# Cross-attention of a decoder layer: both batches of a tile taken together, in halves of the TensorE array

## The chip, the cores and the metric

The kernel runs on one core of a Trainium2 chip. The metric is device time in microseconds (us) of one execution. The engines are named as the profile names them: PE (TensorE, its weight loads as PEld), DVE (VectorE), ACT (ScalarE), POOL (GpSimd), SP (the queue that issues DMAs).

## The reference, cut to what matters

`x` and `ctx` are (32, 64, 512): 32 batches of 64 channels and 512 positions. Three sublayers follow each other, each `x = layernorm(x + f(x))` over the last axis: an attention over batches (called "messages" below), a cross-attention, and a feed-forward network (FFN) with fake-quantised weights and activations. The change is in the second:

```
qh = einsum('bcn,oc->bon', x1, Wq)   # (b, 8 heads, 64, 512)
kh = einsum('bcn,oc->bon', ctx, Wk)
vh = einsum('bcn,oc->bon', ctx, Wv)
qh = softmax(qh, axis=-2) * SCALE    # over the 64 entries of a head
kh = softmax(kh, axis=-1)            # over the 512 positions
context = einsum('bhdn,bhen->bhde', kh, vh)
out = einsum('bhde,bhdn->bhen', context, qh)      # -> (b, 512, 512)
out = einsum('bcn,oc->bon', out, Wo) + bo         # -> (b, 64, 512)
y = out / max(sqrt(sum(out*out, axis=1)), 1e-12) * g * sqrt(64)
x2 = layernorm(x1 + y)
```

## The kernel before

Everything is kept in SBUF. `xt` holds x as 16 tiles (T = 16) of 128 partitions, which are the 64 channels of two batches, by 512 positions. The kernel is written as one instruction list for each engine, in an order set by hand; semaphores (`then_inc`, `wait_ge`) tie the lists. An engine takes its list strictly in order, so what stands behind a waiting instruction waits too.

The stages are: loads and quantisation of the FFN's weights; messages, into which the rest of the weight work is woven; cross-attention; FFN.

Cross-attention goes batch by batch: `slot(b, par, t)` handles batch b (half `par` of tile t) in a loop over t of two slots. While batch b is finished, the logits of batch b+1 are made. The steps of one batch:

- `logits` makes, for each of four 128-row pieces i, key logits into bank i % 2 (L1204) and query logits into bank 4 + i % 2 (L1211). The weights of the keys are padded with zeros, so that all 128 partitions of `ctxs` go through the array although only one batch counts. The query side is fp16 in two parts: `x1p` holds a high and a low half of x1 on the two partition halves, `Wq2` the same of Wq. To get x1 there, `keep_x1` copies it, four DMAs (L388) spread it over the partitions (`x1d`), `high_x1` and `split_x1` (L465) make the parts.
- `maxima` on DVE: negated key maximum (L705), query maximum for each head (L709), subtraction into `EQ` (L712). `exps` on ACT: key exponential with its sum (L960), query exponential (L963). `q_sum` (L718) and one reciprocal (L722) on DVE, `norm_p` on POOL (L475).
- `transpose_k` (L1223) and `transpose_p` (L1234) turn EK and EQ in 128x128 blocks through banks 2 and 3; `copy_k` and `copy_p` on ACT bring them to `ET` and `PTs`.
- `a_product` (L1240) = ctx times ET, over 4 pieces; ACT copies one half of the rows to `ATs`. G = ATs times `Bs` (Wo and Wv multiplied ahead) in L1301; `scale_g` (L742) divides by the key sums.
- `y_product` (L1247) makes y with the positions on the partitions, 64 columns at a time; `bias_y`, `norm_y` (POOL), `sum_y`; `transpose_y` (L1255, L1270) turns y of both batches back and `add_y` (L749) adds it to the tile.
- Layer norms: `ln_stats` (L688, L689) and `ln_apply` (L695) on DVE, the power on POOL. x2's quantisation for the FFN (`scale_x`, `quantize_x`) is woven in; `keep_xq` copies its result.

Of the kernel before, what the change touches and what calls it, by code (L numbers as in the profile page):

```python
# [8 lines left out]
ALU = mybir.AluOpType  # L9
# [42 lines left out]
def decoder_kernel(nc, x, ctx_in, Wq, Wk, Wv, Wo, bo, g, w_gate, w_up, w_down, out):  # L52
# [21 lines left out]
    with ExitStack() as stack:  # L74
# [33 lines left out]
        AREA = 29264  # L108
# [67 lines left out]
        xqn = cut(L // 2).bitcast(BF16)  # L176
# [15 lines left out]
        shift = cut(1)  # L192
        neg_mean = cut(1)
        zero = cut(1)
# [5 lines left out]
        s.q_max_ready = sem("q_max_ready")  # L200
        s.q_max_transposed = sem("q_max_transposed")
        s.q_scales_ready = sem("q_scales_ready")
        s.q_scales_spread = sem("q_scales_spread")
        s.q_scales_copied = sem("q_scales_copied")
        s.q_scaled = sem("q_scaled")
        s.q_high_ready = sem("q_high_ready")
        s.q_low_ready = sem("q_low_ready")
# [31 lines left out]
        s.ln_rstd = sem("ln_rstd")  # L239

        s.x1_ready = sem("x1_ready")
        s.x1n_ready = sem("x1n_ready")
        s.x1d_loaded = sem("x1d_loaded")
        s.x1_high_ready = sem("x1_high_ready")
        s.x1_split = sem("x1_split")
        s.ctx_loaded = sem("ctx_loaded")
# [10 lines left out]
        s.kT_ready = sem("kT_ready")  # L257
        s.kT_copied = sem("kT_copied")
# [4 lines left out]
        s.pqT_ready = sem("pqT_ready")  # L263
        s.pqT_copied = sem("pqT_copied")
        s.y_ready = sem("y_ready")
        s.y_biased = sem("y_biased")
        s.y_squared = sem("y_squared")
        s.y_ss = sem("y_ss")
        s.y_normed = sem("y_normed")
        s.yT_ready = sem("yT_ready")  # L270
        s.x2_added = sem("x2_added")
        s.x2_ready = sem("x2_ready")

        s.x_scaled = sem("x_scaled")
        s.x_shifted = sem("x_shifted")
        s.xqn_ready = sem("xqn_ready")
# [42 lines left out]
        def x1_index(t):  # L319

            return 1 if isinstance(t, int) and t == 0 else 2 * t

        def x2_index(t):

            return 2 * T - 2 if isinstance(t, int) and t == T - 1 else 2 * t + 1

# [9 lines left out]
        def _(sp):  # L336
# [3 lines left out]
            sp.dma_start(wkn[:, :, C:2 * C], Wk.rearrange("(t p) c -> p t c", p=P)).then_inc(s.small_loaded, 16)  # L340
            sp.dma_start(wvn, Wv.rearrange("(t p) c -> p t c", p=P)).then_inc(s.small_loaded, 16)
            sp.dma_start(won, Wo).then_inc(s.small_loaded, 16)
            sp.dma_start(bo_all[:], bo.rearrange("(a c) -> a c", a=1).to_broadcast([P, C])).then_inc(s.small_loaded, 16)
            for h in range(2):
                sp.dma_start(g8[C * h:C * h + C, :], g.rearrange("a c b -> (a c) b")).then_inc(s.small_loaded, 16)
# [38 lines left out]
            def load_x1d(t):  # L384
                sp.wait_ge(s.x1n_ready, t + 1)
                for b in range(2):
                    for h in range(2):
                        sp.dma_start(x1d[C * h:C * h + C, b], x1n[C * b:C * b + C]).then_inc(s.x1d_loaded, 16)  # L388
            sp.dma_start(ctxs, ctx_tok[0]).then_inc(s.ctx_loaded, 16)
            load_x1d(0)  # L390
            with sp.Fori(1, T) as t:
                load_x1d(t)
                sp.wait_ge(s.klog_ready, 8 * t)
                sp.wait_ge(s.ctxT_ready, t)
                sp.dma_start(ctxs, ctx_tok[t]).then_inc(s.ctx_loaded, 16)
# [6 lines left out]
        def _(pool):  # L402
# [9 lines left out]
            pool.memset(wkn[:, :, 0:C], 0.0).then_inc(s.consts, 1)  # L412
            pool.memset(wkn[:, :, 2 * C:3 * C], 0.0).then_inc(s.consts, 1)
            pool.memset(ones[:], 1.0).then_inc(s.consts, 1)
            pool.wait_ge(s.small_loaded, 16 * 8)
# [24 lines left out]
            pool.wait_ge(s.q_high_ready, 1)  # L440
            pool.tensor_tensor(Wq2[:, 1], Wqs[:], Wq2[:, 0], ALU.subtract).then_inc(s.q_low_ready, 1)
# [14 lines left out]
            def ln_rsqrt(n):  # L456

                pool.wait_ge(s.ln_var, n + 1)
                ch.link(pool.tensor_tensor(vare[:], mv[:, 1:2], eps_tile[:], ALU.add))
                pool.tensor_tensor(rstd[:], vare[:], minus_half[:, 0:1], ALU.pow).then_inc(s.ln_rstd, 1)  # L460

            def split_x1(b, par):

                pool.wait_ge(s.x1_high_ready, b + 1)
                pool.tensor_tensor(x1p[C:P, par], x1d[C:P, par], x1p[C:P, par], ALU.subtract).then_inc(s.x1_split, 1)  # L465

                pool.wait_ge(s.x1_split, b + 1)

            def norm_p(b, par):

                pool.wait_ge(s.q_rec_ready, b + 1)
                for i in range(NT):
                    e = EQ[:, par, i].rearrange("p (h d) -> p h d", d=DH)
                    r = qsum[:, par, HEADS * i:HEADS * (i + 1)].unsqueeze(2).to_broadcast([P, HEADS, DH])
                    pool.tensor_tensor(e, e, r, ALU.mult).then_inc(s.p_ready, 1)  # L475
# [7 lines left out]
            def norm_y(b, par):  # L483

                y = Ysb[:, :, C * par:C * par + C]
                pool.wait_ge(s.y_biased, b + 1)
                pool.tensor_tensor(Ysq, y, y, ALU.mult).then_inc(s.y_squared, 1)
                pool.wait_ge(s.y_ss, b + 1)
                ch.link(pool.tensor_tensor(yrn, yss, minus_half[:], ALU.pow))
                pool.tensor_tensor(y, y, yrn.unsqueeze(2).to_broadcast([P, NT, C]), ALU.mult).then_inc(s.y_normed, 1)  # L490

            def slot(b, par, t, front=True, y=True):
                ahead = par == 0 and not (isinstance(t, int) and t == T - 1)
                if ahead:
                    ln_rsqrt(x1_index(t))
                if y:
                    norm_y(b - 1, 1 - par)
                if par == 1 and not (isinstance(t, int) and t == 0):  # L500
                    shift_x(t - 1)

                if not y:
                    pool.wait_ge(s.ln_rstd, x1_index(t) + 1)
                elif par == 0 or (isinstance(t, int) and t == 0):
                    pool.wait_ge(s.y_normed, b)
                else:
                    pool.wait_ge(s.x_shifted, t)
                if not (isinstance(t, int) and t == T - 1):
                    split_x1(b + 2, par)  # L510
                if par == 0 and y:
                    ln_rsqrt(x2_index(t))
                if front:
                    norm_p(b + 1, 1 - par)
            ln_rsqrt(0)
            pool.wait_ge(s.ln_rstd, 1)
            for b in range(2):
                split_x1(b, b)
            norm_p(0, 0)
            slot(0, 0, 0, y=False)  # L520
            slot(1, 1, 0)
            with pool.Fori(1, T - 1) as t:
                ch.enter(t - 1, 4)
                slot(2 * t, 0, t)
                slot(2 * t + 1, 1, t)
            ch.leave(T - 2)
            slot(2 * T - 2, 0, T - 1)
            slot(2 * T - 1, 1, T - 1, front=False)
            norm_y(2 * T - 1, 1)


            def ln_shift(t):
# [27 lines left out]
        def _(dve):  # L560
# [126 lines left out]
            def ln_stats(src):  # L687
                ch.link(dve.bn_stats(st6[:], src), alone=True)  # L688
                dve.bn_aggr(mv[:], st6[:]).then_inc(s.ln_var, 1)  # L689
# [716 lines left out]
```

## Time and profile before

| | |
|---|---|
| median of 3 runs | 1008.78 us (1008.75 to 1013.59) |
| span of the profiled execution, first to last instruction | 1010.8 us |
| busy over the span | PE 80%, DVE 75%, ACT 56%, POOL 43% |
| mean granted clock of TensorE | 0.894 of full |
| messages' and weights' stages end, cross-attention starts | 213.6 us |
| first matmul of the FFN | 801.67 us |
| longest pause of PE after that | 815.2 to 822.6 us, until the first hidden tile is quantised |

The profiled execution's span is 2.0 us above the median of the timed runs and inside their range. In the rows below times are in us from the span's start, "x4" counts instructions that a row merges, and the bracket at a row's end is idle time of the engine just before it, with what ended it. "128*32" of a matmul is rows by columns of the array in use.

### The profile page before, as it was taken

To read this page: it belongs to the slowest core of one execution; us is meant where nothing else is said; L and a number is where in the kernel's file an instruction comes from. 1 tells how busy PE (TensorE), PEld (TensorE's weight loads), DVE (VectorE), ACT (ScalarE), POOL (GpSimd) and SP (SyncE) were. 2 spreads that over 40 slices of the span, in tenths; PEclk is the share of its full clock that TensorE was granted. 3 is DMA by queue.
4 is the path that set the end of the run, shared out by engine and by line. 5 is a ranking of instruction groups with operands and counts; after the bars stand their busy time and mean duration, and the time that the engine had idled before them with its cause. 6 is when DMAs were issued, how large, how long until landed. Compare 5 with 4: busy or idle time off the path is not lost.

```text
span 1010.8 us, 17612 instructions
## 1 busy us (share of the span) xinstructions
PE 809.3 (80%) x5463; PEld 545.3 (54%) x5463; DVE 759.0 (75%) x1660; ACT 568.5 (56%) x1051; POOL 437.1 (43%) x491
## 2 busy tenths in 40 slices
PE   2115555548999999999999999999999867778873
PEld 2104555524767676676766667676667633333331
DVE  3766777748788888888888888888888266666663
ACT  1119777636666666766666676666667223333332
POOL 4423333313445455454545545454553334444443
PEclk7557676659999999999999999999999789999997
DMA  8993111101001101101100110110010000000000
GB/s 201 204 200 137 32 31 31 37 21 32 14 19 31 22 9 31 31 1 30 31 21 10 31 31 0 31 31 21 10 31 1 1 1 30 23 21 21 21 21 31
DMA packets 30372, 38.77 MB, mean 38 GB/s; under 512 B 4496, under 2 KB 16784, under 8 KB 30352
## 3 DMA queue, kind: packets, MB, share of 16 engines
q1 hardware_dynamic: 30352, 38.51, 15.9%
q8 instruction: 12, 0.20, 0.1%
q14 instruction: 8, 0.07, 0.0%
HBM read 25.92 MB, written 4.19 MB: 30 GB/s over the span
## 4 chain that ended last, share of the span: by engine, by line
PE 58%; issue 14%; POOL 8%; DMA 8%; DVE 6%; ACT 5%; SPq 1%; POOLq 0%; ACTq 0%; DVEq 0%
PE bank L1247 11%; PE bank L1204 11%; PE bank L1240 11%; PE bank L1223 5%; PE bank L1170 5%; PE bank L1211 5%; ACT big L873 4%; PE bank L1234 4%; DMA big<-in_ctx_dram 4%; POOL big L545 3%; POOL rstd L540 3%; DMA big<-in_L_ffn_w_down_dram 2%; PE bank L1301 2%; DMA big<-in_L_ffn_w_up_dram 2%; DVE big L565 1%
## 5 line engine op out<-in xcount | busy, mean ns | idle before, releaser
L873 ACT ACTIVATE big<-bank 128x512 f32<-128x512 f32 (+4 forms) x368 | 195.3, 588 | 53.1 <-PE bank L1223 31.5
L475 POOL TENSOR_TENSOR big<-big 128x512 f32<-128x512 f32 x128 | 131.5, 1057 | 81.1 <-DVE big L722 81.1
L1204 PE MATMUL bank<-big,WkT 128*128 128x512 f32 x256 | 136.2, 614 | 13.0 <-DMA big<-in_ctx_dram 8.8
L873 ACT ACTIVATE big<-big 32x256 f32<-32x256 f32 (+6 forms) x160 | 120.3, 772 | 15.6 <-DVE big L766 9.9
L963 ACT ACTIVATE big<-big,q_scales 128x512 f32<-128x512 f32 x128 | 92.4, 722 | 64.3 <-DVE big L712 64.3
L960 ACT ACTIVATE big<-bank,big 128x512 f32<-128x512 f32 x128 | 87.7, 685 | 68.6 <-DVE big L705 67.5
L1247 PEld LDWEIGHTS bank<-big 128*128 128x128 f32 x1024 | 120.6, 194 | 5.6 <-DVE big L742 1.2
L1247 PE MATMUL bank<-big 128*128 128x64 f32 x1024 | 119.4, 275 | 1.0 <-DVE big L742 1.0
L1240 PE MATMUL bank<-big 128*128 128x512 f32 x256 | 116.7, 598 | 0.5 <-ACT big L873 0.5
L718 DVE TENSOR_REDUCE big<-big 128x8 f32<-128x512 f32 x128 | 87.1, 680 | 25.7 <-ACT big L963 24.7
L705 DVE TENSOR_REDUCE big<-bank 128x1 f32<-128x512 f32 x128 | 88.2, 689 | 17.5 <-PE bank L1204 14.4
L1170 PE MATMUL bank<-big 128*128 128x128 f32 x256 | 55.9, 407 | 54.5 <-ACT big L873 54.5
L712 DVE TENSOR_TENSOR big<-bank,big 128x512 f32<-128x512 f32 x128 | 88.5, 691 | 6.9
L709 DVE TENSOR_REDUCE big<-bank 128x8 f32<-128x512 f32 x128 | 87.0, 680 | 7.4 <-PE bank L1211 7.4
L465 POOL TENSOR_TENSOR big<-big 64x512 f16<-64x512 f32 x32 | 37.0, 1157 | 116.1 <-ACT big L873 116.0
L1073 ACT ACTIVATE big<-big,rstd 128x512 f32<-128x512 f32 x16 | 13.0, 812 | 125.1 <-POOL big L541 125.1
L1211 PE MATMUL bank<-Wq,big 128*128 128x512 f16 x256 | 76.7, 381 | 7.2 <-POOL big L465 7.2
L1170 PEld LDWEIGHTS bank<-big 128*128 128x128 f32 x256 | 51.6, 308 | 56.6 <-issue 32.9
L545 POOL TENSOR_TENSOR big<-big 128x1376 f32<-128x1376 f32 x16 | 40.1, 2508 | 93.5 <-DVE big L569 93.5
L1240 PEld LDWEIGHTS bank<-big 128*128 128x128 f32 x256 | 47.4, 190 | 54.3 <-issue 41.6
L1234 PEld LDWEIGHTS bank<-ident,big 128*128 128x128 f32 x512 | 59.7, 140 | 23.5 <-issue 16.9
L565 DVE TENSOR_REDUCE big<-big 128x43 f32<-128x1376 f32 (+2 forms) x42 | 46.6, 1109 | 31.1 <-DMA big<-in_L_ffn_w_down_dram 21.6
(116 smaller groups left out, 1406.1 us busy)
## 6 DMA issues: line engine op xcount, KB each, us to landing
big<-big SPq DMA_DIRECT2D x64, 128.0 KB, 2.3
big<-in_x_dram SPq DMA_DIRECT2D x2, 2048.0 KB, 17.3
big<-in_x_dram SPq DMA_DIRECT2D x4, 1024.0 KB, 11.2
xt<-in_x_dram SPq DMA_DIRECT2D x1, 4096.0 KB, 15.0
big<-in_ctx_dram SPq DMA_DIRECT2D x16, 256.0 KB, 2.7
out_dram<-big SPq DMA_DIRECT2D x16, 256.0 KB, 2.0
big<-in_L_ffn_w_down_dram SPq DMA_DIRECT2D x4, 688.0 KB, 6.7
big<-in_L_ffn_w_gate_dram SPq DMA_DIRECT2D x10, 256.0 KB, 2.7
```

The source lines that it names most:

```text
L475: pool.tensor_tensor(e, e, r, ALU.mult).then_inc(s.p_ready, 1)
L705: dve.tensor_reduce(kneg[:, par, i:i + 1], bank[i % 2][:], X, ALU.max, negate=True).then_inc(s.k_max_ready, 1)
L712: dve.tensor_tensor(EQ[:, par, i].rearrange("p (h d) -> p h d", d=DH), q, qmax[:, par, i].unsqueeze(2).to_broadcast([P, HEADS, DH]), ALU.s ...
L873: return act.activation(dst, src, ACT.Copy)
L960: act.activation(EK[:, par, i], bank[i % 2][:], ACT.Exp, bias=kneg[:, par, i:i + 1], accum_out=ksum[:, par, i:i + 1]).then_inc(s.k_exp_don ...
L963: act.activation(EQ[:, par, i], EQ[:, par, i], ACT.Exp, scale=q_scales[:, 1:2]).then_inc(s.q_exp_done, 1)
L1170: last = pe.matmul(bank[4 + 2 * k + a][:, P * l:P * l + P], qs[:, k, CL // 2 * a + l].rearrange("m h c -> m (h c)"), pd[:, k, CL // 2 * a ...
L1204: pe.matmul(bank[i % 2][:], WkT[:, par, P * i:P * i + P], ctxs, start=True, stop=True).then_inc(s.klog_ready, 1)
L1211: last = pe.matmul(bank[4 + i % 2][:], x1p[:, par, P * i:P * i + P], Wq2[:, part], start=(part == 0), stop=(part == 1))
L1234: last = pe.transpose(bank[2 + j % 2][:, P * i:P * i + P], EQ[:, par, i, P * j:P * j + P], ident[:])
L1240: return pe.matmul(bank[6][:], ctxT[:, i], ET[:, i], start=(i == 0), stop=(i == NT - 1))
L1247: last = pe.matmul(bank[6][:, C * i:C * i + C], PTs[:, j, P * i:P * i + P], GTs[:, j], start=(j == 0), stop=(j == NJ - 1))
```

## The change

- One pass of the loop takes both batches of a tile; the loop over tiles is written out (t from -1 to T-1; f = t + 1 is the tile whose logits are made while tile t is finished).
- Key and query logits of batch 0 use rows 0 to 63 of the array, of batch 1 rows 64 to 127, into different banks (0 to 3, shared by keys and queries). A and y products, and the spreading of the norms, use column halves of one bank; G uses 64x64 quarters.
- Query logits are fp32 and read `xt` directly. The copies, DMAs, splits and the scaling of Wq go.
- y is made with channels on the partitions (x1's layout): GTs is the stationary operand, 512 positions stream. Bias is added on ACT. Squares on POOL, their sums over channels by four matmuls with a 0/1 matrix (`halves`), the power on POOL, and 1/norm is spread over the partitions by eight matmuls; `norm_y` is one DVE operation, the addition to x1 goes to POOL.
- `ctxs` has two buffers; reciprocals of the query sums are made in quarters; quantised x is written straight to `xqb`.

The core of the diff (new functions, then the order on the four engines):

```
+            def k_logits(f, i):
+                if i == 0:
+                    pe.wait_ge(s.ctx_loaded[f % 2], 16 * (f // 2) + 16)
+                if i >= 2:
+                    pe.wait_ge(s.k_exp_done, 8 * f + 2 * i - 2)
+                elif f:
+                    pe.wait_ge(s.q_shifted, 8 * f - 2 + 2 * i)
+                for par in range(2):
+                    rows = slice(C * par, C * par + C)
+                    pe.matmul(bank[2 * (i % 2) + par][:], WkT[rows, P * i:P * i + P], ctxs[rows, f % 2],
+                              start=True, stop=True).then_inc(s.klog_ready, 1)
+            def q_logits(f, i):
...
+                if i >= 2:
+                    pe.wait_ge(s.q_shifted, 8 * f + 2 * i - 2)
+                else:
+                    pe.wait_ge(s.k_exp_done, 8 * f + 6 + 2 * i)
+                for par in range(2):
+                    rows = slice(C * par, C * par + C)
+                    pe.matmul(bank[2 * (i % 2) + par][:], xt[rows, f, P * i:P * i + P], WqT[rows, :],
+                              start=True, stop=True).then_inc(s.qlog_ready, 1)
+            def a_product(f, i):
...
+                pe.wait_ge(s.tr_copied, 16 * f + 2 * i + 2)
+                for par in range(2):
+                    rows = slice(C * par, C * par + C)
+                    last = pe.matmul(bank[6][rows, :], ctxT[:, i, rows], ET[:, par, i],
+                                     start=(i == 0), stop=(i == NT - 1))
+            def g_product(t):
+                pe.wait_ge(s.at_copied, t + 1)
...
+                for j in range(NJ):
+                    for h in range(2):
+                        for par in range(2):
+                            rows, cols = slice(C * par, C * par + C), slice(C * h, C * h + C)
+                            last = pe.matmul(bank[7 - par][cols, C * j:C * j + C],
+                                             ATs[rows, P * j + C * h:P * j + C * h + C], Bs[rows, j, cols],
+                                             start=True, stop=True)
+            def y_product(t):
+                pe.wait_ge(s.gt_copied, 2 * t + 2)
+                pe.wait_ge(s.tr_copied, 16 * t + 16)
+                for j in range(NJ):
+                    for par in range(2):
+                        last = pe.matmul(bank[6][C * par:C * par + C, :], GTs[:, par, j], PTs[:, par, j],
+                                         start=(j == 0), stop=(j == NJ - 1))
+            def sum_squares(t):
+                pe.wait_ge(s.y_squared, t + 1)
...
+            def spread_rn(t):
+                pe.wait_ge(s.y_rn, t + 1)
...
+            def exp_k(f, i):
+                if f and i == 0:
+                    act.wait_ge(s.tr_ready, 16 * f - 8)
+                    act.wait_ge(s.gt_copied, 2 * f)
```

The order of each engine in one pass, as the new loops have it (one line for each engine; k, q, tk, tp, a, ek, eq, ck, cp with their piece):

```
PE:   k0 k1 tp(0,0) G k2 tp(0,1) k3 tp(1,0) tp(1,1) transpose_ctx y_product(t)
      q0 q1 tk0 tk1 sum_squares(t) q2 tk2 a0 q3 tk3 a1 a2 a3 spread_rn(t)
ACT:  ek0 cp0 ek1 cp1 ek2 cp2 ek3 cp3 copy_ctxT bias_y(t) eq0 ck0 eq1 ck1 eq2 ck2 eq3 ck3 copy_ATs
DVE:  kmax0 norm_y(t-1) scale_g(t) kmax1 x1_stats(f) kmax2 ln_apply(f) x2_stats(t-1) kmax3
      ln_apply(t-1) scale_x(t-1) qshift0 qshift1 qsum0 clamp(t) qshift2 qsum1 quantize_x(t-1) qshift3 qsum2 qsum3
POOL: add_y(t-1) rsqrt(x1 of f) rsqrt(x2 of t-1) square_y(t) norm_p0 shift_x(t-1) rsqrt_y(t) norm_p1 norm_p2 norm_p3
```

Every k, q, tk, a, kmax, qshift, qsum, ek, eq, ck, norm_p stands for both batches; tp and cp take one batch and two of its four column blocks. Behind the loop DVE does `norm_y`, `x2_stats`, `ln_apply` and `scale_x` of the last tile ahead of `hidden(0)`, where before it did them after it.

## Rows read from the trace of the kernel before

**Rows 1.** Busy time by stretch: engines with instruction counts, granted clock, DMA share, GB/s.

```profile
core 0: us, PE busy (x) PEld busy (x) DVE busy (x) ACT busy (x) POOL busy (x), PEclk, DMA share, GB/s
100.00:150.00 50.00, 29.06 (x505) 26.80 (x504) 38.28 (x110) 39.91 (x56) 17.27 (x19) 0.67 0.11 32
238.00:802.00 564.00, 550.73 (x3157) 382.56 (x3158) 471.83 (x1007) 374.76 (x733) 270.52 (x326) 1.00 0.09 21
801.60:1010.80 209.20, 153.84 (x800) 74.51 (x800) 132.02 (x287) 65.24 (x130) 90.03 (x86) 0.89 0.05 20
```

**Rows 2.** Timeline of DVE: the addition of y in two successive tiles.

```profile
706.28 0.75 DVE L749 SCALAR_TENSOR_TENSOR xt<-bank,g,xt 128x512 f32 x1 [0.45 <-PE bank L1255]
...
741.73 0.75 DVE L749 SCALAR_TENSOR_TENSOR xt<-bank,g,xt 128x512 f32 x1 [0.44 <-PE bank L1255]
```

**Rows 3.** Groups by line and shape: busy us, mean ns of one, idle before.

```profile
L1204 PE MATMUL bank<-big,WkT 128*128 128x512 f32 x256 | 136.2, 614 | 13.0 <-DMA big<-in_ctx_dram 8.8 <-ACT big L873 1.9 <-ACT wuT L873 1.3
...
L1247 PE MATMUL bank<-big 128*128 128x64 f32 x1024 | 119.4, 275 | 1.0 <-DVE big L742 1.0
...
L1211 PE MATMUL bank<-Wq,big 128*128 128x512 f16 x256 | 76.7, 381 | 7.2 <-POOL big L465 7.2
```

**Rows 4.** Timeline of PE: matmuls on parts of the array, merged.

```profile
23.52 1.61 PE L1123 MATMUL bank<-wg_area 64*64 64x64 f32 x32 [0.47 <-ACT wg_area L873]
...
94.82 0.76 PE L1159 MATMUL bank<-big 128*32 128x32 f32 x64 [0.57 <-ACT big L873]
```

**Rows 5.** Timeline of PE: G's products on 64 rows, then 128 rows again.

```profile
725.69 1.16 PE L1301 MATMUL bank<-Bs,big 64*128 64x128 f32 x8
...
726.77 1.12 PE L1204 MATMUL bank<-big,WkT 128*128 128x512 f32 x2
```

**Rows 6.** Timeline of all engines within one tile: steps and hand-overs.

```profile
717.59 1.08 ACT L873 ACTIVATE big<-bank 128x512 f32<-128x512 f32 x2 [0.49 <-PE bank L1223]
...
720.21 0.69 DVE L705 TENSOR_REDUCE big<-bank 128x1 f32<-128x512 f32 x1
...
720.82 0.68 DVE L709 TENSOR_REDUCE big<-bank 128x8 f32<-128x512 f32 x1
...
720.94 0.69 ACT L960 ACTIVATE big<-bank,big 128x512 f32<-128x512 f32 x1 [2.26 <-DVE big L705]
...
721.52 0.19 ACT L960 ACTIVATION_READ_ACCUMULATOR big<-bank,big 128x1 f32 x1
721.53 0.69 DVE L712 TENSOR_TENSOR big<-bank,big 128x512 f32<-128x512 f32 x1
...
722.26 0.72 ACT L963 ACTIVATE big<-big,q_scales 128x512 f32<-128x512 f32 x1 [0.55 <-DVE big L712]
...
723.43 1.02 PE L1204 MATMUL bank<-big,WkT 128*128 128x512 f32 x2
...
724.49 0.69 DVE L705 TENSOR_REDUCE big<-bank 128x1 f32<-128x512 f32 x1 [0.79 <-PE bank L1204]
...
728.83 0.69 DVE L718 TENSOR_REDUCE big<-big 128x8 f32<-128x512 f32 x1
...
729.55 0.35 DVE L722 RECIPROCAL big<-big 128x32 f32<-128x32 f32 x1
```

**Rows 7.** Timelines of ACT, PE and DVE at the end of the stage.

```profile
790.59 2.81 ACT L873 ACTIVATE big<-bank 128x512 f32<-128x512 f32 x5 [3.22 <-PE bank L1234]
...
791.24 1.15 PE L1234 MATMUL bank<-ident,big 128*128 128x128 f32 x8 [0.25 <-ACT big L873]
792.35 1.16 PE L1301 MATMUL bank<-Bs,big 64*128 64x128 f32 x8
...
793.61 0.88 DVE L742 TENSOR_TENSOR big<-bank,big 64x256 f32<-64x256 f32 x2 [1.32 <-PE bank L1301]
...
794.54 5.29 PE L1247 MATMUL bank<-big 128*128 128x64 f32 x32 [1.04 <-DVE big L742]
```

**Rows 8.** Timelines: first query logits on DVE, first FFN matmuls on PE.

```profile
224.00 0.69 DVE L709 TENSOR_REDUCE big<-bank 128x8 f32<-128x512 f32 x1 [7.24 <-PE bank L1211]
...
801.67 1.78 PE L1335 MATMUL bank<-wg_area,big 128*128 128x480 bf16 x4 [0.69 <-ACT big L873]
```

More of the change, by code:

```diff
@@ L382, in _ @@
                 load_gu(GU, w, src[(FT - 1) * P:FFN, :])
[L384 to L395, printed above, removed]
+            for t in range(T):
+                if t >= 2:
+                    sp.wait_ge(s.klog_ready, 8 * t - 8)
+                    sp.wait_ge(s.ctxT_ready, t - 1)
+                sp.dma_start(ctxs[:, t % 2], ctx_tok[t]).then_inc(s.ctx_loaded[t % 2], 16)
             with sp.Fori(0, T) as t:
@@ L494, in slot @@
[L494 to L500, printed above, removed]
-                    shift_x(t - 1)
[L503 to L529, printed above, removed]
+            def square_y(t):
+                pool.wait_ge(s.y_biased, t + 1)
+                if t:
+                    pool.wait_ge(s.y_summed, t)
+                pool.tensor_tensor(Ysq, Ysb, Ysb, ALU.mult).then_inc(s.y_squared, 1)
@@ L788, in slot @@
                     scale_x(t - 1)
                 if front:
-                    maxima(f, fp, 2)
-                    q_sum(f, fp, 2)
-                if even and y:
-                    add_y(t - 1)
+                    q_shift(f, 0)
+                    q_shift(f, 1)
+                    q_sum(f, 0)
+                if back:
+                    clamp_ss(t)
                 if front:
-                    maxima(f, fp, 3)
-                if even and y:
-                    x2_stats(t - 1)
@@ new lines, in exp_q, with copy_k @@
+            def exp_q(f, i):
+                for par in range(2):
+                    act.wait_ge(s.q_shifted, 8 * f + 2 * i + par + 1)
+                    act.activation(EQ[:, par, i], EQ[:, par, i], ACT.Exp).then_inc(s.q_exp_done, 1)
+            def copy_k(f, i):
+                if f and i == 0:
+                    act.wait_ge(s.at_ready, f)
+                for par in range(2):
+                    n = 16 * f + 2 * i + par
+                    act.wait_ge(s.tr_ready, n + 1)
+                    copy(ET[:, par, i], bank[4 + n % 2][:]).then_inc(s.tr_copied, 1)
@@ L1304, in _ @@
-            pe.wait_ge(s.q_low_ready, 1)
-            for i in range(NT):
-                logits(0, 0, 0, i)
-            slot(0, 0, 0, y=False)
-            slot(1, 1, 0)
-            with pe.Fori(1, T - 1) as t:
-                slot(2 * t, 0, t)
-                slot(2 * t + 1, 1, t)
-            slot(2 * T - 2, 0, T - 1)
-            slot(2 * T - 1, 1, T - 1, front=False)
-            y_product(2 * T - 1)
+                    last = pe.matmul(bank[7][:, 2 * i:2 * i + 2], Ysq[:, P * i:P * i + P], halves[:],
+                                     start=True, stop=True)
```

696 lines of the change are left out of this document (295 added, 401 removed).

## The prediction

> **What bounds the kernel now.** First the busy time by stretch [rows 1]. From 238 to 802 us the cross-attention runs, 16 tiles of two batches each, and TensorE is busy for 550.7 of 564 us at the full clock; VectorE has 84%, ScalarE 66%. One tile, from one `add_y` to the next, takes 741.73 - 706.28 = 35.45 us [rows 2]. So TensorE sets this stage and VectorE follows at some 30 us a tile. Before it (messages) TensorE is busy 58% of the time at a granted clock of 0.67, behind it (FFN) 74% at 0.89 [rows 1]: the reader is to keep this pair in mind, because the clock is full only where TensorE hardly pauses.
>
> **What a tile costs TensorE.** One fp32 product with 512 columns is two instructions; a pair lasts 1.02 us [rows 6], a single one 0.60 to 0.61 [rows 3], so each adds 0.43 to its predecessor and the product 0.86. Per tile before: 8 key logits 6.9, 8 fp16 query logits (two fp16 instructions each, at half an fp32 step, 0.21) 3.4, 64 + 4 transposes at 0.11 (eight in 1.15 with a tail [rows 7]) 7.5, 8 A products 6.9, two y products at 3.7 (32 instructions each; the busy time of all 1024 is 119.4 us, 0.117 each with little idle [rows 3]) 7.4, G 1.8, y's transposes 0.4. Sum 34.3, with the changes of array mode 35: the measured turn.
>
> **The halves.** Do two products in different halves of the array run at once? No row shows it with 512 columns. Two rows show it with fewer: 64 instructions of 32 columns in four column groups take 0.76 us, where at 0.84 ns a column (0.43 us / 512) they would take 1.72 in sequence, and 32 instructions of 64 columns on 64x64 parts take 1.61 with a tail of 0.31, against 1.72 even at full clock [rows 4]. Bounds for a pair of 512 columns: 0.86 (at once) and 1.72 us (in sequence). I take 0.86, nearest to these rows. The price is the change of mode: from the first K=64 matmul to the first K=128 one 1.08 us pass where eight steps of 0.11 make 0.87, and the next pair takes 1.12 instead of 1.02 [rows 5]: 0.2 us a change, of which the new order has some 16 a tile.
> TensorE after, at full clock: keys 3.4, queries 3.4 (fp32, so nothing is won), transposes 7.5, A 3.4, y 3.4, G 0.5 to 1, squares' sums 0.9, spreading of 1/norm 0.9, changes 3.2: 27 us. All in sequence it would be 40.
> The Trainium skill (TensorEngine Tiling (Array Packing), PSUM Bottleneck) says that tiling speeds up TensorE but not the evacuation of PSUM, which may become the limit. By it the evacuating engine would set the turn: with the 29.2 us of VectorE worked out below that is 15 x 6.2 = 93 us less, with the ends some 935; by the ring that I walk below, more than before. The sum does without the rule.
>
> **VectorE and ScalarE after.** VectorE's steps start to start [rows 6]: key maximum 0.61, query maximum 0.71, subtraction 0.61, sum 0.72. Eight of each: 21.2 us. Reciprocals in quarters (0.2 to 0.35 each) add 0.9, the two `scale_g` 0.9 + 0.2, both layer norms 2.6, quantising x 2.5, `norm_y` 0.7, clamp 0.15. Sum 29.2 us. Bias, `sum_y`, half of the additions and the carrier memsets are gone, some 2 us. ScalarE: key exponential with its accumulator read 0.58 + 0.13 to 0.19, copy 0.49, query exponential 0.63 to 0.72: about 21 us. POOL some 14 us. Were each engine's own work the limit, a turn would last 29 to 30 us.
>
> **But the new order is a ring.** I follow one turn from S, the start of the last query subtraction of tile f-1 (`q_shift(f-1,3)`):
> 1. ScalarE has `copy_k(3)` behind `exp_q(3)`: hand-over 0.73 [rows 6], exponential 0.63, first copy 0.49: second copy at 1.85; from a copy to TensorE 0.65 (790.59 to 791.24 [rows 7]) 2.5.
> 2. TensorE: `a_product(3)` 0.86, `spread_rn` 0.86, mode 0.2, key logits 0 and 1 1.72, mode 0.2: 6.35; transposes of P 0.87, mode 0.2: 7.4. P is normalised by about 5.4 on POOL, not late. ATs is copied by 4.2.
> 3. G 0.5, hand-over 0.4 (the whole step was 1.26 with eight serial instructions [rows 7]), `scale_g` twice 0.45 and to ScalarE 0.05: 9.25. `exp_k(f,0)` waits for this, since it overwrites ksum.
> 4. ScalarE alternates two exponentials and two copies of P, 2.4 to 2.5 us, four times. Last copy starts 18.5.
> 5. `y_product` waits for all copies: 0.65 + 3.43, mode 0.2: 22.8. Only behind it stand the query logits: hand-over 1.06 (723.43 to 724.49 [rows 6]): VectorE starts at 23.9.
> 6. VectorE to the next S without a wait: seven subtractions and eight maxima 10.0, two sums with reciprocals 3.3, clamp 0.15, quantising 1.3: 14.7.
> Turn: 38.6 us at full clock. VectorE waits 9.4 of it: 1.4 for key logits 0, 1 for G, 0.7 for key logits 2, 6.3 for query logits 0, which before lay among its other work. So a stall goes from TensorE to VectorE. The waiting `y_product` has the query logits behind it, and these have all of VectorE's second half.
>
> **The clock.** In that turn TensorE pauses 3.3 us ahead of `a_product(3)`, 2.3 ahead of key logits 2, and from 14 to 19 it has only transposes. Busy share 27 / 38.6 = 70%. The two stages with 58% and 74% had 0.67 and 0.89 [rows 1], and the last y product of before, behind pauses of only 0.25 and 1.04, took 5.29 instead of the 3.7 us above [rows 7]. I take 0.82: about 36% of the time at 1.2 GHz. The path holds 9 us of TensorE (steps 2, 3, 5), so 3.4 us more; bounds 0 and 9 (all at half speed). Turn 42.0.
>
> **Ends.** Start of the stage: the four DMAs of x1d and the fp16 split go, behind which VectorE waited 7.2 us for its first query logits at 224.0 [rows 8]. By the same steps at half clock the new first S is at about 238. Tile 0's turn has no quantising, `spread_rn` and norm: 36.4 + 3.4. Fourteen turns follow: 238 + 39.8 + 14 x 42.0 = 866. Then the last tile's tail: transposes, y, bias, squares, sums, power 1.0, spreading, all in TensorE's order ahead of the FFN, some 22 us: first `gate_up` at 888, before at 801.7 [rows 8]: +86. Back come 4 us: the 7.4 us pause at 815 (table ahead) was for x2's norm of the last tile, now done before `hidden(0)`. Loads and messages are untouched; the four small DMAs more run under the weights. Span 1010.8 + 82 = 1092.8. The span lies 2.0 above the median of the runs, so the time is 1008.8 + 82, about 1090 us.
>
> **Rivals.**
> *Ring at full clock* (17%): 38.6 us a turn, 3.4 x 15 = 51 us less than above: 1040. For it: TensorE never rests wholly for longer than 3.3 us; against it the FFN's rows.
> *Halves in sequence* (10%): on the path `a_product`, `spread_rn`, two key logits, y and G double: +7.3 us a turn at full clock, 15 turns: 1150, above that with a lower clock. Rows 4 speak against it.
> *VectorE's own work decides* (12%): the wait for query logits 0 is filled or shorter than I walk it, so that VectorE idles under 35.45 - 29.2 = 6.2 us a turn. That is the point where it turns. It asks that steps 1 to 5 take 3.2 us less, say by a ScalarE alternation of 8.6 (exponentials of 0.58 with the read hidden) together with hand-overs of half my size. A turn of 32.5 gives 45 us less than before, with the ends at +20: 985.
> *Cancelling out* (4%): a turn of 34.5 to 35 and the ends: within 0.5%.
> The forecast itself has 57%: turn 40.5 to 44, 1065 to 1125.
>
> **Numbers.** A measurement of this kernel tells about 0.5% (5 us) from no change. Slower: 57 + 17 + 10 = 84%; the same 4%; faster 12%. The range for 8 in 10 takes in the full clock and most of the serial case and leaves out the faster one: 1010 to 1155.
>
> **What would show it.** In the profile of the changed kernel: (a) two matmuls of key logits starting within some 10 ns and a pair of pairs in about 1.05 us; else the halves are in sequence. (b) VectorE idle 5 to 8 us ahead of the first query maximum of each tile, ended by TensorE. (c) ScalarE's first key exponential waits for `scale_g`. (d) TensorE's busy share near 70% and granted clock 0.75 to 0.9 between 240 and 860 us. (e) the turn about 42 us. It is wrong if VectorE is over 85% busy in the stage, or if the clock stays at 1.00.

## The result and the profile after

The changed kernel takes 1089.5 us (four executions, 1084.3 to 1097.2) beside 1011.2 (1008.8 to 1014.0) for the kernel before on the same chip: 1.078 times as long (1.072 to 1.084), slower, at the predicted 1090. The profiled execution has a span of 1083.9 us.

From the page of the changed kernel: busy time, TensorE's granted clock in 40 slices, and the shares of the chain that ended last.

```profile
PE 743.1 (69%) x5249; PEld 426.7 (39%) x5264; DVE 722.1 (67%) x1460; ACT 506.5 (47%) x985; POOL 395.4 (36%) x410
...
PEclk9998667589999889898988899889888789999897
...
PE 31%; DVE 28%; ACT 15%; issue 14%; POOL 8%; DMA 4%; ACTq 1%; SPq 0%; POOLq 0%; DVEq 0%
```

No engine bounds it: the busiest has 69%, and the chain changes hands between TensorE, VectorE and ScalarE. That is what a ring looks like on a page. Busy time by stretch says where, the second line beside the 238 to 802 us of [rows 1]:

```profile
core 0: us, PE busy (x) PEld busy (x) DVE busy (x) ACT busy (x) POOL busy (x), PEclk, DMA share, GB/s
100.00:150.00 50.00, 29.02 (x504) 26.85 (x504) 37.57 (x109) 38.98 (x55) 16.85 (x18) 0.70 0.11 32
298.62:836.32 537.70, 407.42 (x2446) 220.59 (x2444) 367.13 (x689) 262.38 (x559) 195.21 (x208) 0.89 0.02 6
889.00:1083.00 194.00, 139.93 (x747) 69.51 (x760) 127.55 (x275) 61.47 (x123) 86.77 (x80) 0.91 0.06 22
```

The messages and the FFN are as they were. In the cross-attention TensorE fell from 98% busy to 76%, VectorE from 84% to 68%, and the clock from 1.00 to 0.89. The stretch from 298.62 to 836.32 is thirteen turns long: it begins and ends 0.4 us ahead of a start of the y bias (L905), so 537.70 / 13 = 41.36 us a turn, where it was 35.45 [rows 2].

One turn, from the y bias at 502.55 to the next at 544.03, from the timelines of all engines, put in order of time; the prediction's S, the last query subtraction, is the row at 520.69. Ahead of it stand the first S of the stage (238.76) and two rows of an earlier turn that the last section reads, behind it the first `gate_up`. L1078 is the query logits, L1089 and L1100 transposes, L1119 A, L1158 the spreading, L1066 the key logits, L1132 G, L1143 y; on VectorE L637 and L640 are query maximum and subtraction, L630 key maximum, L661 `scale_g`, L695 the quantising product; on ScalarE L864 is the key exponential, L905 the y bias, and L435 on POOL normalises the probabilities. L781 is any copy on ScalarE, and on VectorE L675 is `norm_y` and L652 the reciprocals of the query sums; L1222 is `gate_up`.

```profile
238.76 0.69 DVE L640 TENSOR_TENSOR big<-bank,big 128x512 f32<-128x512 f32 x1
...
474.92 0.69 DVE L695 TENSOR_TENSOR big<-big 128x512 bf16<-128x512 fp8e4 x1
474.99 2.53 POOL L435 TENSOR_TENSOR big<-big 128x512 f32<-128x512 f32 x2
...
502.55 0.69 ACT L905 ACTIVATE big<-bank,bo 128x512 f32<-128x512 f32 x1 [3.35 <-PE bank L1143]
503.60 0.69 DVE L637 TENSOR_REDUCE big<-bank 128x8 f32<-128x512 f32 x1 [5.79 <-PE bank L1078]
507.54 1.61 PE L1089 MATMUL bank<-ident,big 128*128 128x128 f32 x8 [2.09 <-ACT big L781]
510.57 2.08 PE L1078 MATMUL bank<-WqT,xt 64*128 64x512 f32 x4
512.68 0.69 DVE L637 TENSOR_REDUCE big<-bank 128x8 f32<-128x512 f32 x1 [1.83 <-PE bank L1078]
517.10 2.54 POOL L435 TENSOR_TENSOR big<-big 128x512 f32<-128x512 f32 x2 [1.78 <-DVE big L652]
517.33 1.41 DVE L695 TENSOR_TENSOR big<-big 128x512 bf16<-128x512 fp8e4 x1
520.69 0.69 DVE L640 TENSOR_TENSOR big<-bank,big 128x512 f32<-128x512 f32 x1
523.07 1.08 PE L1119 MATMUL bank<-big 128*64 128x512 f32 x4 [3.44 <-ACT big L781]
523.98 1.04 PE L1158 MATMUL bank<-ident,big 128*64 128x128 f32 x16
524.96 1.99 PE L1066 MATMUL bank<-big,WkT 64*128 64x512 f32 x8
526.11 1.29 DVE L630 TENSOR_REDUCE big<-bank 128x1 f32<-128x512 f32 x2 [1.58 <-PE bank L1066]
526.87 1.09 PE L1100 MATMUL bank<-ident,big 128*128 128x128 f32 x8
528.21 0.69 PE L1132 MATMUL bank<-Bs,big 64*64 64x64 f32 x32 [0.24 <-DVE big L675]
529.04 0.76 DVE L661 TENSOR_TENSOR big<-bank,big 128x256 f32<-128x256 f32 x2 [0.87 <-PE bank L1132]
529.88 0.69 ACT L864 ACTIVATE big<-bank,big 128x512 f32<-128x512 f32 x1 [5.08 <-DVE big L661]
531.38 1.65 PE L1066 MATMUL bank<-big,WkT 64*128 64x512 f32 x4 [2.48 <-ACT big L864]
532.96 1.97 PE L1100 MATMUL bank<-ident,big 128*128 128x128 f32 x8
540.34 3.65 PE L1143 MATMUL bank<-big 128*64 128x512 f32 x16 [1.31 <-ACT big L781]
543.92 1.56 PE L1078 MATMUL bank<-WqT,xt 64*128 64x512 f32 x6
544.03 0.69 ACT L905 ACTIVATE big<-bank,bo 128x512 f32<-128x512 f32 x1 [3.35 <-PE bank L1143]
...
879.91 1.78 PE L1222 MATMUL bank<-wg_area,big 128*128 128x480 bf16 x4 [0.69 <-ACT big L781]
```

Read it downwards from 520.69: each pause in square brackets is ended by another engine, and most of those had themselves come late because of a third. VectorE's pauses, by the view of waits over thirteen turns (total, times, longest; L1150 is the sums of squares, L669 the clamp that reads them):

```profile
DVE big L637 <- PE bank L1078: 88.1, 20, 6.1
DVE big L630 <- PE bank L1066: 59.1, 38, 4.3
DVE big L661 <- PE bank L1132: 11.6, 13, 1.2
DVE big L669 <- PE bank L1150: 1.5, 4, 0.5
```

160.3 / 13 = 12.3 us a turn. The work that TensorE was spared became waiting of VectorE for TensorE.

### The profile page after: what moved, and what is told of

It is laid out like the page before. It is cut to its first block, busy times and chain, and to the rows that moved or that the text cites. A ratio compares the mean times of both kernels' runs of the same rounds, so it can differ in the third digit from the quotient of the medians.

```text
span 1083.9 us, 15238 instructions
## 1 busy us (share of the span) xinstructions
PE 743.1 (69%) x5249; PEld 426.7 (39%) x5264; DVE 722.1 (67%) x1460; ACT 506.5 (47%) x985; POOL 395.4 (36%) x410
## 4 chain that ended last, share of the span: by engine, by line
PE 31%; DVE 28%; ACT 15%; issue 14%; POOL 8%; DMA 4%; ACTq 1%; SPq 0%; POOLq 0%; DVEq 0%
ACT big L781 9%; DVE big L637 7%; PE bank L1066 5%; PE bank L1143 5%; DVE big L640 5%; PE bank L1029 5%; ACT big L864 4%; DVE big L649 3%; PE bank L1078 3%; DVE big L513 3%; PE bank L1100 3%; POOL big L496 3%; POOL rstd L491 3%; DMA big<-in_L_ffn_w_down_dram 2%; PE bank L1158 2%
## 5 line engine op out<-in xcount | busy, mean ns | idle before, releaser
L781 ACT ACTIVATE big<-bank 128x512 f32<-128x512 f32 (+3 forms) x352 | 188.7, 596 | 48.8 <-PE bank L1119 23.8
L435 POOL TENSOR_TENSOR big<-big 128x512 f32<-128x512 f32 x128 | 137.0, 1097 | 167.6 <-DVE big L652 167.6
L637 DVE TENSOR_REDUCE big<-bank 128x8 f32<-128x512 f32 x128 | 87.1, 681 | 104.4 <-PE bank L1078 104.4
L870 ACT ACTIVATE big<-big 128x512 f32<-128x512 f32 x128 | 80.6, 630 | 148.9 <-DVE big L640 148.9
L864 ACT ACTIVATE big<-bank,big 128x512 f32<-128x512 f32 x128 | 87.4, 697 | 92.7 <-DVE big L661 87.3
L630 DVE TENSOR_REDUCE big<-bank 128x1 f32<-128x512 f32 x128 | 82.2, 684 | 69.0 <-PE bank L1066 68.9
L1066 PE MATMUL bank<-big,WkT 64*128 64x512 f32 x256 | 86.9, 785 | 39.6 <-ACT big L864 38.3
L1089 PE MATMUL bank<-ident,big 128*128 128x128 f32 x512 | 81.7, 310 | 41.2 <-ACT big L781 41.2
L1119 PE MATMUL bank<-big 128*64 128x512 f32 x256 | 71.5, 660 | 46.7 <-ACT big L781 46.7
L1089 PEld LDWEIGHTS bank<-ident,big 128*128 128x128 f32 x512 | 62.6, 156 | 90.0 <-ACT big L781 65.6
L640 DVE TENSOR_TENSOR big<-bank,big 128x512 f32<-128x512 f32 x128 | 88.5, 691 | 4.4
L781 ACT ACTIVATE big<-big 32x256 f32<-32x256 f32 (+4 forms) x112 | 90.3, 833 | 1.1
L649 DVE TENSOR_REDUCE big<-big 128x8 f32<-128x512 f32 x128 | 86.3, 674 | 2.2
L1100 PE MATMUL bank<-ident,big 128*128 128x128 f32 x512 | 82.8, 313 | 5.9 <-ACT big L781 5.8
L1100 PEld LDWEIGHTS bank<-ident,big 128*128 128x128 f32 x512 | 64.6, 159 | 54.7 <-issue 24.8
L1078 PE MATMUL bank<-WqT,xt 64*128 64x512 f32 x256 | 75.6, 689 | 0.1
L1029 PEld LDWEIGHTS bank<-big 128*128 128x128 f32 x256 | 52.6, 313 | 56.5 <-issue 36.6
L1143 PE MATMUL bank<-big 128*64 128x512 f32 x256 | 58.5, 597 | 20.4 <-ACT big L781 20.4
L496 POOL TENSOR_TENSOR big<-big 128x1376 f32<-128x1376 f32 x16 | 40.3, 2516 | 88.1 <-DVE big L517 88.1
L943 ACT ACTIVATE big<-big,shift,rstd 128x512 f32<-128x512 f32 x16 | 13.0, 813 | 125.3 <-POOL shift L492 125.3
L513 DVE TENSOR_REDUCE big<-big 128x43 f32<-128x1376 f32 (+2 forms) x42 | 46.6, 1109 | 32.4 <-DMA big<-in_L_ffn_w_down_dram 22.6
```

The lines of the kernel that those rows point to most:

```text
L637: ch.link(dve.tensor_reduce(qmax[:, i, par], q, X, ALU.max))
L640: dve.tensor_tensor(EQ[:, par, i].rearrange("p (h d) -> p h d", d=DH), q, qmax[:, i, par].unsqueeze(2).to_broadcast([P, HEADS, DH]), ALU.s ...
L649: last = dve.tensor_reduce(qsum[:, i, par], EQ[:, par, i].rearrange("p (h d) -> p h d", d=DH), X, ALU.add)
L781: return act.activation(dst, src, ACT.Copy)
L864: act.activation(EK[:, par, i], bank[2 * (i % 2) + par][:], ACT.Exp, bias=kneg[:, par, i:i + 1], accum_out=ksum[:, par, i:i + 1]).then_inc ...
L1029: last = pe.matmul(bank[4 + 2 * k + a][:, P * l:P * l + P], qs[:, k, CL // 2 * a + l].rearrange("m h c -> m (h c)"), pd[:, k, CL // 2 * a ...
```

## The experiments

My theory after the result: the ring of the prediction sets the turn, and the pauses it puts into TensorE cost it clock. Rivals: VectorE's own work decides after all; TensorE's work is longer than I reckoned; the clock has no part in it. All kernels below are the changed one with the edit shown. Line numbers on TensorE and ScalarE move by a few with an edit. "Turn" is from one y bias to the next, a mean over the steady part. The profiled execution gives turns and rows, the median of four or five the time.

**1. Query logits ahead of y.** VectorE's largest wait, 5.79 us at 503.60, should shrink if the waiting y product is what holds the query logits.

```
-                y_product(t)
                 q_logits(f, 0)
                 q_logits(f, 1)
+                y_product(t)
```

> TensorE's list has q_logits 0 and 1 ahead of y_product instead of behind it; nothing else. Ring theory (the order of the lists sets the turn): the first query maximum starts 5 us earlier, right behind ctx's transposes; then query logits 2, still behind transpose_k(1) and sum_squares, come late, so that 2 to 3 us of the 5 are left. Turn 41.4 to 38.5-39.5 us, time 1045 to 1062. Rival (an engine's own work or slow halves set the turn, the order does not matter): 1085 to 1095.

Measured: 1037.4 us, 1.025 of before (1.020 to 1.029); turn 38.8 us, clock 0.92. The wait that stood at 5.79 falls to 1.00, and two small ones are new, here on VectorE's timeline, since the squares' sums and query logits 2 now stand further behind y:

```profile
524.07 0.69 DVE L637 TENSOR_REDUCE big<-bank 128x8 f32<-128x512 f32 x1 [1.00 <-PE bank L1078]
...
532.76 0.17 DVE L669 TENSOR_SCALAR big<-bank 128x8 f32<-128x8 f32 x1 [1.23 <-PE bank L1150]
...
533.81 0.69 DVE L637 TENSOR_REDUCE big<-bank 128x8 f32<-128x512 f32 x1 [0.89 <-PE bank L1078]
```

It follows that step 5 of the ring is real: the query logits waited for y. The turn is in the expected range, the time 8 us below it. Up to 1 us of the 2.5 a turn can be the clock, if its rise from 0.89 to 0.92 is priced by experiment 3, where 0.89 to 1.00 is worth 3.6 (an estimate).

**2. The first steps shortened.** ScalarE copies the last transposes ahead of its last query exponentials, G stands ahead of the transposes of P, `norm_y` ahead of the key maximum.

```
-  for i in range(NT): exp_q(f, i); copy_k(f, i)
+  for i in range(2): exp_q(f, i); copy_k(f, i)
+  for i in range(2, NT): copy_k(f, i); exp_q(f, i)
...
-  transpose_p(t, 0, 0); g_product(t)
+  g_product(t); transpose_p(t, 0, 0)
...
-  k_max(f, 0); norm_y(t - 1)
+  norm_y(t - 1); k_max(f, 0)
```

> ScalarE copies K's transposes 2 and 3 ahead of query exponentials 2 and 3; TensorE does G ahead of transpose_p(0,0); VectorE does norm_y ahead of the key maxima. Ring theory: steps 1 to 3 (from the last query subtraction to the first key exponential) fall from 9.9 us to about 7.5, turn 39 us, time 1050 to 1065. Rival (y's wait and the query side alone decide, the front of the ring is covered): 1085 to 1095.

Measured: 1029.5 us, 1.017 (1.012 to 1.022); turn 37.2, clock 0.91. That is a larger gain than expected (turn 39, 1050 to 1065 us). VectorE's timeline shows that the wait behind y stays as it was, and its wait for key logits falls from 4.5 to about 1.3 us a turn, so the gain came from steps 1 to 3:

```profile
519.23 0.69 DVE L637 TENSOR_REDUCE big<-bank 128x8 f32<-128x512 f32 x1 [5.78 <-PE bank L1081]
```

**3. Pauses filled.** Nothing is moved; TensorE gets matmuls that nobody reads (fp32, 512 columns, into a free bank): three ahead of A 3, two ahead of the second transposes of the keys, one each ahead of key logits 2 and of y, with waits of their own (left out here) until the bank that they overwrite is free. If only the clock changes, the turn is the ring at full clock.

```
+            def fill(b, n):
+                for _ in range(n):
+                    pe.matmul(bank[b][:], ident[:], WkT[:], start=True, stop=True)
```

> The changed kernel with fp32 matmuls of 512 columns that nobody reads put into four pauses of TensorE's list (3 ahead of a_product(3), 2 ahead of transpose_k(1), 1 each ahead of key logits 2 and y). Clock theory: the granted clock in the stage rises from 0.89 to 0.97 or more and the turn falls from 41.4 to 39-40 us: time 1055 to 1075. Rival (the clock is not on the path; the added matmuls only delay): clock or no clock, 1090 to 1110.

Measured: 1037.9 us, 1.026 (1.021 to 1.030), 52 us less than the changed kernel, though it does more, and less than the 1055 to 1075 expected. Thirteen turns, 490.40 / 13 = 37.72 us each, at a clock of 1.00; the windows and the same turn from the timelines:

```profile
300.70:791.10 490.40, 436.79 (x2630) 217.01 (x2628) 359.77 (x689) 259.19 (x559) 194.65 (x208) 1.00 0.02 7
```

```profile
528.40 0.69 DVE L637 TENSOR_REDUCE big<-bank 128x8 f32<-128x512 f32 x1 [6.04 <-PE bank L1078]
...
542.66 0.69 DVE L640 TENSOR_TENSOR big<-bank,big 128x512 f32<-128x512 f32 x1
...
545.04 1.08 PE L1119 MATMUL bank<-big 128*64 128x512 f32 x4
...
546.93 1.99 PE L1066 MATMUL bank<-big,WkT 64*128 64x512 f32 x8
548.84 1.09 PE L1100 MATMUL bank<-ident,big 128*128 128x128 f32 x8
...
550.17 0.69 PE L1132 MATMUL bank<-Bs,big 64*64 64x64 f32 x32 [0.24 <-DVE big L675]
...
551.85 0.69 ACT L864 ACTIVATE big<-bank,big 128x512 f32<-128x512 f32 x1 [5.08 <-DVE big L661]
...
561.34 3.65 PE L1143 MATMUL bank<-big 128*64 128x512 f32 x16 [0.45 <-ACT big L781]
```

**4. Only the longest pause filled, and only the others.** The three matmuls ahead of A 3 alone; then the other four alone.

```
-  fill: 3 ahead of a_product(f, 3), 2 ahead of transpose_k(f, 1), 1 ahead of k_logits(f, 2), 1 ahead of y_product(t)
+  first kernel:  3 ahead of a_product(f, 3)
+  second kernel: 2 ahead of transpose_k(f, 1), 1 ahead of k_logits(f, 2), 1 ahead of y_product(t)
```

> Only the 3.4 us pause ahead of a_product(3) is filled (the three matmuls of e4), the other pauses stay. If this one long pause costs the clock, the stage's clock comes near the 1.00 of e4 and the turn near 37.7 us: 1040 to 1050. If the cold stretches come from the many shorter pauses and the stretches of transposes, most of the loss stays: turn 40 to 41, 1070 to 1085.

> The reverse: the four other matmuls of e4 (2 ahead of transpose_k(1), 1 each ahead of key logits 2 and y), the pause ahead of a_product(3) stays. If the long pause alone costs the clock: 1075 to 1090. If the others do: 1040 to 1055.

Measured: with the longest pause filled 1047.4, 1065.6, 1067.8 and 1083.3 us, too far apart for a ratio; the profiled execution, the longest of the four, has turns of 37.7 to 41.9 and a clock of 0.91. With the others filled 1044.6 us, 1.032 (1.028 to 1.037), turn 37.85, clock 0.99, though a long pause ahead of A 3 is still there, now of 2.73 us where the changed kernel had 3.44:

```profile
505.33 1.08 PE L1119 MATMUL bank<-big 128*64 128x512 f32 x4 [2.73 <-ACT big L781]
```

So with the shorter pauses (1.3 to 2.5 us) filled, the clock is all but full and nearly the whole gain is there; the longest need not be filled for it. What filling the longest alone is worth stays open, with executions from 1047 to 1083 us.

**5. y half by half.** The loops of `y_product` are swapped: first all eight instructions of one batch, then those of the other.

```
-  for j in range(NJ):
-      for par in range(2):
+  for par in range(2):
+      for j in range(NJ):
```

> y_product's two loops are swapped: the four matmuls of batch 0 (columns 0 to 63) first, then the four of batch 1; same work. If only neighbours in the list run at once, y takes 7 us instead of 3.65 and lies fully on the ring: turn +3.4, time 1135 to 1145. Rival (each half has its own queue and runs ahead of the other): y stays at 3.6 us, time 1085 to 1095.

Measured: 1127.4 us, 1.115 (1.110 to 1.120); turn 43.7.

```profile
608.49 5.39 PE L1143 MATMUL bank<-big 128*64 128x512 f32 x16 [1.31 <-ACT big L781]
```

The group of sixteen instructions took 5.39 us, neither the 3.6 of halves that run at once nor the 7 of a sequence. So halves overlap only partly when the instructions of one half stand together, and y's length is on the ring: 1.74 us more there are 2.3 us more a turn, part of which may be the clock (0.87 instead of 0.89).

**6. Quantising moved.** `quantize_x` goes from between VectorE's query steps to ahead of them, into its wait, to test step 6.

```
-  quantize_x(t - 1)   # ahead of q_shift(f, 3)
...
   scale_x(t - 1)
+  quantize_x(t - 1)
```

(POOL's `shift_x` goes ahead of `square_y` for it.)

> The changed kernel with quantize_x ahead of the query maxima, where VectorE waits 5.8 us for y, instead of between q_shift(2) and q_shift(3); POOL's shift_x ahead of square_y. Ring theory: its 1.75 us leave the ring: turn 41.4 to 39.6, time 1060 to 1068. Rival (VectorE's total decides, wherever its work stands): 1085 to 1095.

Measured: 1064.6 us, 1.055 (1.050 to 1.060), 25 us less than the changed kernel. The windows of three and of eight successive turns of one execution:

```profile
298.30:410.90 112.60, 85.91 (x568) 45.72 (x566) 83.65 (x159) 60.16 (x129) 43.69 (x48) 0.95 0.02 8
491.00:818.70 327.70, 264.20 (x1508) 140.09 (x1506) 224.64 (x424) 162.12 (x344) 116.47 (x128) 0.83 0.02 6
```

The same instructions take 112.60 / 3 = 37.5 us a turn at a clock of 0.95 and 327.70 / 8 = 41.0 at 0.83. Over thirteen turns the mean is 40.0 instead of 41.4. How much of that is the step taken off the ring and how much the clock, this run can't tell: the clock alone moves the turn by more than the edit.

**7. Query logits ahead of y, respaced.** Kernel 1 with its two new waits removed: query logits 2 ahead of the second transposes on TensorE, and the clamp one step later on VectorE.

```
   transpose_k(f, 0)
+  q_logits(f, 2)
   transpose_k(f, 1)
   sum_squares(t)
-  q_logits(f, 2)
...
-  clamp_ss(t)
   q_shift(f, 2)
+  clamp_ss(t)
```

> e1 with query logits 2 moved ahead of transpose_k(1) and sum_squares in TensorE's list, and VectorE's clamp behind q_shift(2): this takes away the 1.2 and 0.9 us that VectorE waits in e1 for the sums and for query logits 2. Ring theory: turn 38.8 to about 36.5 us, time 1000 to 1010. Rival (e1 took what was to be had): 1030 to 1040.

Measured: 981.4 us, 0.969 (0.966 to 0.973); turn 34.4, clock 0.95. Expected was 1000 to 1010 and a turn of 36.5; the clock rose too, which I hadn't counted.

**8. Both.** Kernels 2 and 7 together, nothing else.

> e1b and e2 together. Ring theory: they shorten different steps, so the gains add: turn 41.4 - 4.2 - 4.9 = 32.3, held up a little where VectorE (29.2 us of own work) gets near its limit: 33 to 34 us, time 965 to 985, faster than the kernel before. Rival (both take away the same wait): turn 36 to 37, time 1005 to 1025.

Measured: 928.1 us (926.0 to 929.2), 0.917 of before (0.914 to 0.920), faster than the kernel before, than kernels 2 and 7 and than expected. Its thirteen turns all last 30.6 us. Its window and VectorE's waits in it:

```profile
289.30:686.70 397.40, 350.23 (x2446) 186.07 (x2444) 358.17 (x690) 253.35 (x559) 193.31 (x208) 1.00 0.03 8
```

```profile
DVE big L637 <- PE bank L1082: 14.0, 13, 1.1
DVE big L630 <- PE bank L1070: 9.5, 13, 0.7
DVE big L649 <- ACT big L871: 4.9, 13, 0.4
```

L1082 is the query logits here, L1070 the key logits, and L649 the query sums, which wait for the query exponentials (L871). A turn is 397.40 / 13 = 30.57 us; VectorE is busy for 90% of it and waits 28.4 / 13 = 2.2 us. TensorE's work is 350.23 / 13 = 26.9 us a turn at full clock, so the change does cut it from 35 to the 27 predicted. The bound is now VectorE, as the rival had it; the same instructions as the changed kernel's, in another order. This is also the cleanest case for the ring: experiment 3 and this kernel both run at a clock of 1.00, and their turns are 37.72 and 30.57 us, so of the 10.8 us between the changed kernel's 41.36 and these 30.57 some 7 are order and 3.6 clock.

**9. Both, filled.** Unread matmuls in kernel 8: two ahead of G, one each ahead of key logits 2 and the second transposes.

```
+  fill(6, 2)  # ahead of g_product(t)
+  fill(6, 1)  # ahead of k_logits(f, 2)
+  fill(6, 1)  # ahead of transpose_k(f, 1)
```

> e3 with matmuls that nobody reads in three pauses (2 ahead of G, 1 ahead of key logits 2, 1 ahead of transpose_k(1)). Clock theory: what is left of cold stretches goes, 0.5 to 1.5 us a turn: 950 to 975. Rival (no pauses left to fill; the added 3.4 us of matmuls lie on the path): slower than e3 by 10 to 40 us.

Measured: 943.1 us, 0.933 (0.930 to 0.937); turn 31.6. That is 15 us more than kernel 8, inside the range of the expectation's rival: the clock was already 1.00, so nothing was to be had, and the turn grew by 1.0 us.

**10. Both, y half by half.** Experiment 5's edit in kernel 8.

> e3 with y's two loops swapped as in e5, which there made y 5.4 instead of 3.65 us and the turn 2.3 us longer. If TensorE's y is still on the ring of e3: turn 30.6 to 32.2, time 950 to 955. If in e3 VectorE's own work covers y (it waits only 0.4 us behind the exponentials that follow y): at most 0.5 us a turn, 928 to 936.

Measured: 958.7 us, 0.946 (0.942 to 0.950), 4 us above the expected range; turn 32.4, 1.85 longer. y took 5.4 us again, and VectorE's wait at its first query sum grew from 0.38 to 2.14 us:

```profile
516.15 5.42 PE L1147 MATMUL bank<-big 128*64 128x512 f32 x16
...
522.92 0.69 DVE L649 TENSOR_REDUCE big<-big 128x8 f32<-128x512 f32 x1 [2.14 <-ACT big L871]
```

A longer y is thus not hidden even where VectorE is 90% busy: in this order it stands between TensorE's query logits and transposes, and ScalarE waits behind it.

## Why the prediction was right

**Halves.** Right. Four instructions of two products take 1.08 to 1.13 us, a single pair took 1.02 [rows 6]; y's sixteen take 3.65, reckoned 3.43 and one change of mode. What the prediction didn't see is that this hangs on alternating the halves (experiments 5 and 10).

**The ring, steps 1 to 6.** Right, each within half a microsecond, if the turn at full clock of experiment 3 is read from S at 542.66: A 3 at +2.38 (2.5 predicted), the transposes behind the first key logits at +6.18 (6.35), G at +7.5 (7.4), ScalarE's first key exponential, ended by `scale_g`, at +9.19 (9.25), y at +18.68 (19.15), and from the first query maximum to the next S 542.66 - 528.40 = 14.26 (14.7). The turn is 37.72 where 38.6 was walked, and the kernel takes 1037.9 where the rival "ring at full clock" had 1040. Experiments 1, 2 and 7 moved work out of one piece of it each, with the same instructions, and the turn fell by 2.5, 4.2 and 7.0 us (1 and 7 on the same piece), the last two by more than the whole clock is worth (3.6). Step 6 is not shown this way, since experiment 6 can't tell it from the clock.

**VectorE.** It waits 12.3 us a turn, and 9.2 in experiment 3; 9.4 was the sum at full clock, so with 3.4 for the clock nearly 12.8. Its own work was reckoned at 29.2 start to start; in kernel 8 the turn without waits is 30.57 - 2.2 = 28.4.

**The clock.** The cost came out, 41.36 - 37.72 = 3.6 us a turn (3.4), but not by the prediction's working, so this is luck. The granted clock is 0.89, not 0.82. And a share of 36% of the time at 1.2 GHz lengthens the 9 us of TensorE's work on the path to 9 / 0.82 = 11.0, by 2.0 us; some 3.2 come out if 36% of the work is slow. At the measured 0.89 an even spread gives 9 / 0.89 - 9 = 1.1 us, a third of what was found. It isn't even, the slow stretches fall where VectorE waits: the transposes at 507.54 took 1.61 us and those at 532.96 1.97, where eight at full clock take 1.09; and query logits 2 at 510.57 took 2.08 and made VectorE wait 1.83 (the whole wait is absent in experiment 3). The walk had step 6 without a wait. Over thirteen turns VectorE waits 59.1 us for key logits (30.0 in experiment 3) and 88.1 for query logits (78.5): 2.2 and 0.7 us a turn. Another 0.4 goes to VectorE's quantising product, in the turns in which query logits 2 are late: see the last section.

**Ends and sum.** First S at 238.76 (238 predicted). The first `gate_up` came at 879.9, not 888: 14 turns of 41.36 instead of 42.0 are 9 us. The FFN's pause until the first hidden tile is quantised fell from 7.4 to 3.3 us, the 4 us expected back; its longest is now one of 5.1 us, which was there before too. The profiled span is so 73 us longer than before's, not 82; this execution lies 3.8 us below the median of its four, and 1089.5 - 1011.2 = 78 us is the difference of medians, where before's own median is now 2.4 above the 1008.8 that the sum started from. So that 1090 was met within 1 us is in part luck; the sum was some 4 to 9 us too long.

**The checks.** (b), (c), (e) came as written: 5.8 us of wait ahead of the first query maximum, `scale_g` ahead of the exponential, 41.4 us a turn. (d) 76% and 0.89: the clock within the 0.75 to 0.9 named, the share above 70% because slow instructions count as busy (TensorE is busy for 31.3 us a turn with the instructions that take 26.9 in kernel 8). For (a) the merged groups show the 1.1 us of a pair of pairs; the starts of single matmuls are not in these views. Neither sign of being wrong appeared.

**The rivals.** Halves in sequence: fell. VectorE decides: fell for this kernel, and its condition (a wait under 6.2 us a turn) is met in kernel 8, which is faster, as it should be. The Trainium skill (TensorEngine Tiling (Array Packing), PSUM Bottleneck) names the evacuation of PSUM as what may become the limit once products are tiled; the trace of kernel 8 agrees, with VectorE 90% busy, that of the changed kernel, with 68%, does not. What I missed there is how near that case was: six small moves away (experiments 1, 2 and 7 hold them). And 985 us was the wrong price for it. I took the ends as 20 us more than before, but in the forecast's own sum they are 16 less: at a turn of 35.45 it gives 238 + 33.25 + 14 x 35.45 + 22 = 790 where before had 801.7, and 4 us come back. By that sum a turn of 32.5 gives 948 us, and kernel 8's 30.57 gives 919, where 928 was measured. The same slip is in "Cancelling out" (a turn of 34.5 to 35 gives 979 to 986 us, faster; kernel 7 with 34.4 took 981) and in the 935 us by the skill's rule (899).

## What to carry to other kernels

When a change cuts the busiest engine's work, walk one turn of the new order before counting the gain: here 8 us a tile of TensorE's work went, and the hand-written order turned it into 6 us more, until six groups of instructions were moved (928 us instead of 1090). Put work that depends on nothing new ahead of a product that waits for the last of many copies, and let the engine in the middle copy what another waits for before it does what nobody waits for yet. Use parts of the array alternately, instruction by instruction, and look at the granted clock after every reordering, since a ring's pauses cost a second time there.

## What the runs showed of the hardware that was not expected

**Unread work made this kernel faster.** Seven unread products a turn took 52 us off the changed kernel (experiment 3), and the four in the shorter pauses were enough for 45 of them (experiment 4). Within one execution the same code ran three turns of 37.5 us and, two turns later, eight of 41.0 (experiment 6).

**Order within the array.** Sixteen instructions on two halves take 3.65 us alternated and 5.4 half by half, with the same operands.

**VectorE and GpSimd on one product.** In the changed kernel the quantising product (L695) takes 0.69 us in six of the thirteen turns and 1.41 in seven, 1.08 on average, and always 0.69 in experiments 3, 6 and 8. In the timeline of the first section, at 474.92, GpSimd starts 0.07 us behind VectorE: VectorE's product takes 0.69 us and the first of GpSimd's two 1.53 instead of 1.04. At 517.10 GpSimd is 0.23 us ahead: its first product takes 1.09, VectorE's 1.41, and GpSimd's second, which starts behind VectorE's, 1.49. GpSimd's pair thus takes 2.53 or 2.54 us in either case, instead of the 2.04 of a pair alone; VectorE loses time only when it is second, and it is second in just the seven turns in which it had waited for query logits 2, as at 512.68. That costs 0.4 us a turn on average in the changed kernel; in experiment 1 every one of ten takes 1.41. The product reads two tensors from SBUF, and the Trainium skill (GPSIMD Engine Reference, Specifications) names contention with just such VectorE instructions; the rows agree, but no run here separates it from other causes.
